# Wide rest keys: twelve 32-row by 32-column products in place of five larger ones, permuted sums, and a rewritten list of entries

## The reference, cut to what matters

```python
logits = jnp.einsum('bhqd,bhkd->bhqk', q, k) * scale + col_bias
probs = jax.nn.softmax(logits, axis=-1)          # over 154 keys
out = jnp.einsum('bhqk,bhkd->bhqd', probs, v)
x = out.reshape(B, HW, 1024) @ Wo + bo + residual
```

## Time and profile before

| | |
|---|---|
| median of 3 runs | 1953.7 us (1947.69 to 1956.24) |
| the profiled execution | 1944.85 us, its span 1942.7 us |
| PE busy | 1779.3 us (92%) |
| DVE, ACT, POOL busy | 1223.8, 1040.1, 416.7 us |
| mean granted PE clock | 0.957 of 2.4 GHz |

### The profile page before, as it was taken

The page is one execution under the profiler, slowest core; times in us unless marked ns, Lnnn a source line. Parts: engine busy times, 40 slices in busy tenths (PEclk is TensorE's granted clock), DMA queues, the critical chain, the costliest instruction groups (busy, mean ns, idle before and its releaser), DMA issues. The chain is left out here.

```text
span 1942.7 us, 27390 instructions
## 1 busy us (share of the span) xinstructions
PE 1779.3 (92%) x9644; PEld 977.8 (50%) x9644; DVE 1223.8 (63%) x2393; ACT 1040.1 (54%) x1761; POOL 416.7 (21%) x299
## 2 busy tenths in 40 slices
PE   6898487999999999999999999899999999999674
PEld 5786334454545454545445545445554545454333
DVE  4457545576767676767666766567666777766332
ACT  1120163666666666666656665566666666666231
POOL 4242302122212121212122211121213121221301
PEclk9997797999999999999999999899999999999786
DMA  8984622051315121512352223322332233221205
GB/s 278 312 289 160 183 63 46 13 97 35 74 41 119 34 73 43 120 35 70 89 119 80 68 59 87 56 72 48 80 70 59 56 79 75 56 58 39 65 19 200
DMA packets 175758, 175.61 MB, mean 90 GB/s; under 512 B 92673, under 2 KB 132157, under 8 KB 173512
## 3 DMA queue, kind: packets, MB, share of 16 engines
q1 hardware_dynamic: 173320, 163.39, 32.5%
q10 hardware_dynamic: 2304, 10.49, 1.4%
HBM read 127.17 MB, written 46.63 MB: 89 GB/s over the span
## 5 line engine op out<-in xcount | busy, mean ns | idle before, releaser
L1181 DVE TENSOR_REDUCE tops<-general 128x2 bf16<-128x308 f32 x1024 | 437.5, 473 | 152.6 <-PE general L1284 91.4
L1141 POOL TENSOR_TENSOR kept<-kept,inv_b 128x512 f32<-128x512 f32 x192 | 246.6, 1305 | 580.1 <-DMA inv_b<-scratch_inverses 580.1
L1044 ACT ACTIVATE probs<-score_ps 128x512 f32<-128x512 f32 x512 | 297.2, 597 | 121.2 <-PE score_ps L1320 109.3
L1168 DVE CAST q_aux<-q_pair 64x512 bf16<-64x512 f32 x160 | 86.6, 541 | 214.6 <-ACT q_pair L1032 213.4
L1031 ACT ACTIVATE q_pair<-general 64x512 fp32r<-64x512 f32 x160 | 94.5, 590 | 194.0 <-PE general L1265 193.5
L1054 ACT ACTIVATE q_aux<-general 4x512 bf16<-4x512 bf16 x320 | 187.3, 585 | 13.6 <-PE general L1291 8.4
L1080 ACT ACTIVATE a_hi<-kept 128x512 fp32r<-128x512 f32 x192 | 110.0, 622 | 154.2 <-POOL kept L1141 94.4
L1214 DVE TENSOR_TENSOR x<-general,x 128x512 f32<-128x512 f32 x160 | 109.1, 691 | 114.4 <-PE general L1363 113.5
L1066 ACT ACTIVATE kept<-out_ps 128x512 f32<-128x512 f32 x192 | 107.6, 595 | 134.1 <-PE sum_ps L1345 91.5
L1129 POOL TENSOR_TENSOR x_lo<-xn,x_hi 128x1024 fp32r<-128x1024 f32 x32 | 75.9, 2372 | 406.2 <-ACT x_hi L1012 280.7
L1280 PE MATMUL general<-w_top,q_aux 128*128 128x154 bf16 x1024 | 128.9, 233 | 23.3 <-DVE q_pair L1171 9.9
(11 more groups left out here) (150 smaller groups left out, 3280.0 us busy)
## 6 DMA issues: line engine op xcount, KB each, us to landing
inv_b<-scratch_inverses SPq DMA_DIRECT2D x128, 256.0 KB
inv_b<-scratch_inverses SPq DMA_DIRECT2D x128, 128.0 KB
xn<-scratch_stream SPq DMA_DIRECT2D x16, 512.0 KB, 3.6
w_pair<-scratch_wk_hi SPq DMA_DIRECT2D x32, 256.0 KB
x<-scratch_stream SPq DMA_DIRECT2D x16, 512.0 KB, 3.3
scratch_stream<-x SPq DMA_DIRECT2D x16, 512.0 KB, 3.8
scratch_wk_hi<-p_kout_hi SPq DMA_DIRECT2D x16, 308.0 KB
p_raw<-in_L_xattn_Wk_dram SPq DMA_DIRECT2D x4, 1024.0 KB, 8.2
```

The costliest lines, as they stand in the source:

```text
L1044: nc.scalar.activation(dst, score_ps[:, number % 2, :], ACT.Exp, scale=scale).then_inc(act_exp.sem, 1)
L1141: last = nc.gpsimd.tensor_tensor(tile, tile, inv_b[:, i, :], ALU.mult)
L1181: last = nc.vector.tensor_reduce(tops[:, n % 2, sub, 2 * pair:2 * pair + 2], src, AX_X, ALU.max)
```

## The change

In `value` with k = 1 of a wide step the order is now: the two `w_val` products, the four sums of 128 rows and 32 columns, and then twelve products that all have 26 rows (of a group of 32) and 32 columns. Eight of them are the former four rest products, each cut into two halves of 32 columns (`side`). Four replace the product of 128 x 128: each adds the rest keys of one head. `SUMS` moves head j's sums to another quarter of `sum_ps`, so that no two of the twelve use the same row group and column group together. The heads now leave `sum_ps` in the order 1, 3, 0, 2, and the read of the inverses is reshaped to fit: it has the same number of rows and bytes, with a stride of 4 rows in place of 8. `sel_rest` shrinks from 4 x 128 to 4 x 32 columns.

```diff
+SUMS = (slice(64, 96), slice(0, 32), slice(96, 128), slice(32, 64))
...
 ORDER = """
-    rest 15, output 2 0, norm 2 1, wkeys 0+ 2, wkeys 0+ 3, value 14 1, score 15 0, low 2 1, score 15 1,
+    rest 15, scale 2 1, output 2 0, score 15 0, max 0+ 2, max 0+ 3, score 15 1, max 0+ 4, norm 2 1,
...
-        sel, sel_rest = sb("sel", [P, 4, 32]), sb("sel_rest", [P, 4, P])
+        sel, sel_rest = sb("sel", [P, 4, 32]), sb("sel_rest", [P, 4, 32])
...
-                        src = dr["inverses"].rearrange("(i h g) n -> g h i n", i=2, h=2)[batch:batch + 1, h]
+                        src = dr["inverses"].rearrange("(h i g) n -> g h i n", h=2, i=2)[batch:batch + 1, 1 - h]
...
-                    last = nc.vector.memset(sel_rest[32 * j:32 * j + REST, g, 32 * j + 8 * g:32 * j + 8 * g + 8], 1.0)
+                    last = nc.vector.memset(sel_rest[32 * j:32 * j + REST, g, 8 * g:8 * g + 8], 1.0)
...
                         if k == 1:
                             for j in range(4):
-                                i, rows = j % 2, slice(32 * j, 32 * j + REST)
-                                nc.tensor.matmul(out_ps[64 * i:64 * i + 64, j // 2, :], w_val_rest[rows, g * DW:(g + 1) * DW], rest[rows],
-                                                 start=False, stop=True, skip_group_check=True)
+                                nc.tensor.matmul(sum_ps[SUMS[j]], sel[:, g, :], probs[:, j, :],
+                                                 start=(g == 0), stop=False, skip_group_check=True)
+                            for side in range(2):
+                                for j in range(4):
+                                    rows, at = slice(32 * j, 32 * j + REST), 64 * (j % 2) + 32 * side
+                                    cols = slice(g * DW + 32 * side, g * DW + 32 * side + 32)
+                                    nc.tensor.matmul(out_ps[at:at + 32, j // 2, :], w_val_rest[rows, cols], rest[rows],
+                                                     start=False, stop=True, skip_group_check=True)
                             for j in range(4):
-                                nc.tensor.matmul(sum_ps[32 * j:32 * j + 32, :], sel[:, g, :], probs[:, j, :],
-                                                 start=(g == 0), stop=False, skip_group_check=True)
-                            last = nc.tensor.matmul(sum_ps[:], sel_rest[:, g, :], rest, start=False, stop=(g == 3), skip_group_check=True)
+                                rows = slice(32 * j, 32 * j + REST)
+                                last = nc.tensor.matmul(sum_ps[SUMS[j]], sel_rest[rows, g, :], rest[rows],
+                                                        start=False, stop=(g == 3), skip_group_check=True)
```

More of the change, by code:

```diff
@@ L511 @@
 ORDER = """
[L512 to L550, removed]
@@ L551 @@
-    rest 15, output 2 0, norm 2 1, wkeys 0+ 2, wkeys 0+ 3, value 14 1, score 15 0, low 2 1, score 15 1,
-        max 0+ 4, scale 2 2, max 0+ 5, max 0+ 6, score 15 2, score 15 3, output 2 1, max 0+ 7, norm 2 2,
-        query 1+ 0, low 2 2, turn 0+, query 1+ 1, scale 2 3, value 15 1
+    rest 0, score 0 0, output 2- 2, score 0 1, max 1 1, score 0 2, max 1 2, max 1 3, score 0 3, norm 2- 3,
+        sums 3- 0, max 1 4, max 1 5, value 0 0, max 1 6, max 1 7, low 2- 3, query 2 0, turn 1, query 2 1,
+        value 0 1, output 2- 3,
@@ new lines @@
+    rest 4, value 3 1, max 5 6, score 4 0, score 4 1, max 5 7, max 6 0, sums 0, output 3- 0, max 6 1,
+        split 2, turn 5, score 4 2, max 6 2, score 4 3, max 6 3, max 6 4, norm 3- 1, max 6 5, inverse 0,
+    rest 5, max 6 6, value 4 1, max 6 7, max 7 0, max 7 1, score 5 0, score 5 1, scale 0 0, max 7 2,
+        turn 6, max 7 3, score 5 2, max 7 4, score 5 3, max 7 5, max 7 6, max 7 7, low 3- 1,
+    rest 6, query 8 0, turn 7, query 8 1, value 5 1, score 6 0, score 6 1, output 3- 1, score 6 2,
+        scale 0 1, max 8 0, score 6 3, max 8 1, max 8 2, norm 0 0,
@@ new lines @@
+    rest 7, max 8 3, max 8 4, value 6 1, low 0 0, score 7 0, score 7 1, max 8 5, max 8 6, output 0 0,
+        scale 0 2, norm 0 1, max 8 7, score 7 2, score 7 3, low 0 1, query 9 0, turn 8, value 7 1,
+        output 0 1, norm 0 2, max 9 0, max 9 1, nkeys 0 0,
+    rest 8, low 0 2, max 9 2, max 9 3, query 9 1, score 8 0, score 8 1, output 0 2, score 8 2, max 9 4,
+        scale 0 3, value 8 0, max 9 5, nkeys 0 1, norm 0 3, max 9 6, score 8 3, max 9 7, low 0 3,
+        query 10 0, turn 9, query 10 1, value 8 1,
@@ new lines @@
+    rest 9, output 0 3, score 9 0, sums 1, max 10 0, score 9 1, max 10 1, squares 3, max 10 2, max 10 3,
+        score 9 2, max 10 4, nkeys 0 2, score 9 3, max 10 5, value 9 0, max 10 6, nkeys 0 3, max 10 7,
+        inverse 1, square 3, query 11 0, query 11 1, turn 10, value 9 1, rate 3, max 11 0, max 11 1,
+    rest 10, max 11 2, score 10 0, max 11 3, max 11 4, max 11 5, score 10 1, max 11 6, max 11 7,
+        score 10 2, score 10 3, early 0+, query 12 0, value 10 0, turn 11, scale 1 0, value 10 1, max 12 0,
+        max 12 1,
@@ L554 @@
+    rest 14, output 1 1, score 14 0, max 15 5, score 14 1, max 15 6, max 15 7, score 14 2, max 0+ 0,
+        wkeys 0+ 2, score 14 3, norm 2 0, turn 15, low 2 0, max 0+ 1, query 0+ 1, value 14 1,
+    rest 15, scale 2 1, output 2 0, score 15 0, max 0+ 2, max 0+ 3, score 15 1, max 0+ 4, norm 2 1,
+        max 0+ 5, score 15 2, max 0+ 6, score 15 3, max 0+ 7, low 2 1, query 1+ 0, turn 0+, value 15 1,
+        wkeys 0+ 3, scale 2 2, output 2 1, norm 2 2, scale 2 3, max 1+ 0, low 2 2, query 1+ 1
 """
```

16 lines of the change are left out of this document (added).

## The result

| | before | changed |
|---|---|---|
| median | 1954.45 us (4 runs) | 1900.78 us (4 runs, 1896.19 to 1904.44) |
| the profiled execution | 1944.85 us, span 1942.7 us | 1896.19 us, span 1893.9 us |

The ratio of changed to before is 0.973, with an interval of 0.9697 to 0.9764. The change takes off about 54 us by the medians and 48.8 us by the two spans. I had predicted 1899 us.

The account below looks back on a forecast made before the run. PE's time for its products was taken to bound the kernel. -58.9 + 1.2 + 3 = -54.7 us, from a median of 1953.7 us, gave 1899 us, range 1884 to 1932 us.

Parts of the forecast that it names:

- The price of the twelve: PE's group of twelve products in wide `value` entries: 1.06 us, so 0.92 us less a step, 58.9 us in all.
- The two-wave rival: Only eight of the twelve overtake: group 1.54 us, gain 28 us, 1930 us; chance 0.18, shared with a half-lost gain.
- the slower rival: Four rest sums take turns at one bank: group 3.6 us, 2060 us; chance 0.08, bad list included.
- (a): The two `value` entries of a wide step stand together in 9 steps in place of 17: +1.2 us.
- (d): Rewritten list at the turn from window to window: costed at nothing, bound 2 us a window, 16 us in all.
- (f): Shorter PE work meets other engines' chains that were just in time: 3 us, between nothing and 24 us.
- (b): Reshaped read of inverses and smaller `sel_rest`: nothing, under 1 us if the cover were gone.
- (c): Shorter `value` entry still covers ACT's `turn`: 1.4 us left, holding with PE there 0.92 us sooner.
- The waits at `rest 0`: Sign in PE's timeline: its waits at `rest 0` should add up to 10 to 25 us.
- (e): Sixteen loads on the SP queue delay everything behind them: PE again waits 8 to 10 us, no change.
- The rival of no gain: Twelve run as three waves, about 1.96 us, or the list gives back 40 us or more: about 1950 us; chance 0.06.

Follow-up runs that it names:

- the list alone: The kernel before with only the new list of entries: 1.0047 of the kernel before.
- the old list: The changed kernel with the list of entries of the kernel before, so the new products alone: 0.9787 of the kernel before, median 1909.06 us.
- the repeat: The changed kernel itself run once more, nothing changed, beside later experiments: 0.9757 of the kernel before.
- POOL's wait: POOL's product `scale` k also waits for DVE's `low` k-1: 0.979 of before on the changed kernel, 0.9936 on the new products with the old list.
- the uncut kernel: The changed kernel with the eight half products put back as four of 26 rows and 64 columns: 1.0029 of the kernel before.

## Why the prediction was right

**The price of the twelve** was the term that decided. I took 1.06 us; the median is 1.045. With the sums' 0.996 the saving is 59.8 us where the sum had 58.9. The two-wave rival at 1.54 us and the slower rival at 3.6 us did not occur: at 828.81 and 828.87 all twelve first halves start, and four row groups that write the one bank of `sum_ps` cost nothing. The Trainium skill, TensorEngine Tiling (Array Packing), section Gotcha 1: PSUM Pressure, says that different row tiles cannot access the same PSUM bank at the same time. Here the measurement differs, and it decides. The doubt behind the rival was sound in another form: products of the same place do take turns, at 0.83 us a group, and products of another size do not overlap. Neither was in my list of unknowns; the change avoids both.

**What is given back** was too small in the sum. Of 59.8 us, 48.8 arrive in the profiled executions, so (a), (d) and (f) are together worth 11 us, and I had 4.2. Of the 11 us, 2.5 are more idle time of PE over the whole span (163.4 to 165.9), and 8.5 stand in its busy time. The list brings this busy time: 1.0 to 1.7 us a window, 9.1 us in the run of the list alone. So the term that was mis-sized is (d), the rewritten list, which I put at nothing; of its cost only the 1.2 us of (a) were in the sum. Why PE needs longer for the same products in the new order stays open. In the window from 606.38 us PE goes 105 times from one shape of product to another where before it did 102 times, but if 4 and 32 columns count as one shape it is 99 times, so the number of changes does not decide it. The term (f), 3 us, fits where the list stays the new one: there 57 of 59.8 us arrive. With the old list 41 us arrive, so 18 us are given back, and my argument that DVE and ACT have time left does not cover that. It counts totals (and put DVE at 139 of 192 us, where the earlier trace rows give 138 and the trace after has 142.73 of 192.58); the waits come from the order on each engine.

By the medians 54 of 59.8 us arrive, and the interval of the ratio, 46 to 59 us, holds both. That the forecast is within 2 us of the median is luck in part: by the spans the saving is 5.9 us less than forecast, and the repeat's 0.9757 makes 1906 us of 1953.7. The total came out right because the terms that were off are small.

**(a)** `w_val` stands as x8 in 9 steps, as the order said. **(b)** holds, PE nowhere waits for the inverses' new read. **(c)**, that the shorter entry still covers ACT's `turn`, holds only with the new list, under which PE's list of waits has no more L1309 for `q_aux`; with the old list it was 19 short ones, so my single place of 1.4 us to spare didn't speak for all steps. **(d)** was wrong as a mechanism, and too small by what the list costs alone. The waits at `rest 0` are one of 7.3 us, where I expected 10 to 25. The new waits are not at the turn but at the output products L1369, 10.0 us in twelve times. And I took the list for harmless by itself: alone it costs 9 us, within the 16 us that I had as a bound, and only beside the new products it is worth 6 to 11. **(e)** was right in kind: everything behind the sixteen loads is late, and PE waits 7.33 us, a little under my 8 to 10.

**The rival of no gain** through the list did not occur in full; the closest to it was the kernel of the new products with the old list and POOL's wait, 0.9936.

## What to carry to other kernels

Small products that are left over can be cut until all have one size and each its own rows and columns of the array: twelve of 26 x 32 then cost what one costs. Check both properties first, since either one missing takes the whole gain. When the engine that bounds the kernel gets faster, run the new work with the old order and the new order with the old work: an order is only good or bad for the lengths that it was made for. Look at busy time as well as at waits then: here the new order cost PE some 9 us of longer work that the view of waits does not show. And two instructions that stretch each other to two or three times their length are not yet worth pulling apart; here neither way of doing so gained any time.

## What the runs showed of the hardware

- Twelve float32 products of 26 rows and 32 columns with different places run as one group of 1.045 us. Eleven later products start ahead of the second half of the first; the twelve first halves all start within 0.08 us.
- Of the same place, a product waits for both halves of the earlier one: 1.877 us. Of another size (26x64, then 26x32), no product overlaps: 2.010 us.
- Four row groups of the array write one bank at the same time at no cost: four products of 26x32 into `sum_ps` take 0.99 us (830.22 to 831.21 in the uncut kernel), as four that share their rows do (0.996 us).
- The clock fell to 1.2 GHz 2.5 us into a wait of 7.33 us and stayed there for 10.2 us; L1309 behind it took 1.94 us in place of 1.07. Shorter waits had it too: with the old list and POOL's wait, six stretches of 3.4 us in mid-run each stand behind a wait of 1.72 us, and 199.2 us are at that level in all. And three stretches of the kernel with the new products and the old list stand behind no wait over 0.17 us, but behind sixteen products of one column.
- POOL and DVE stretch each other: 1.29 us to 3.34 for two subtractions, 0.42 to 1.41 for a cast, 2.53 to 2.97 for POOL's product.
